# Opening of a three-part attention and expert kernel: loads reordered, queries of the first tile alone, the other three tiles' queries as units of the first batch

## The reference, cut to what matters

```
x = x + cross_attention(layernorm(x), ctx)    # x: 8 batches x 64 queries x 256; ctx: 8 x 1601 x 256; 16 heads of 16
x = x + causal_self_attention(layernorm(x))   # 64 tokens of each batch
x = x + experts(layernorm(x))                 # 8 experts of 256 -> 1024 -> 256, the best 2 of each token
q = layernorm(x) @ Wq.T + bq;  k = ctx @ Wk.T + bk;  v = ctx @ Wv.T + bv
cross_attention = (softmax(q k / 4) v) @ Wo.T + bo
```

## Time and profile before

| | |
|---|---|
| runs before | 703.81, 708.26, 1222.36 us; median 708.26 |
| profiled execution, its own time | 710.84 us |
| its span in the trace | 709.0 us, 16064 instructions |
| PE, DVE, ACT, POOL busy | 94%, 67%, 46%, 41% of the span |
| mean granted TensorE clock | 0.976 of full |

### The profile page before, as it was taken

How to read it: one execution, slowest core, us unless ns; L and a number is a source line. 1 busy time by engine, 2 the same in 40 slices (tenths; PEclk the granted TensorE clock), 3 DMA queues, 4 the chain that set the end, 5 groups by cost and what they waited for, 6 DMA issues and landing times.

```text
span 709.0 us, 16064 instructions
## 1 busy us (share of the span) xinstructions
PE 663.4 (94%) x6584; PEld 544.1 (77%) x6584; DVE 476.0 (67%) x868; ACT 324.3 (46%) x520; POOL 290.8 (41%) x384
## 2 busy tenths in 40 slices
PE   2979999999999999999999999888997999999997
PEld 2657877877877877877887886655786999999996
DVE  4695677657567887674977865667764766666753
ACT  2434554554554455455445544345444444444421
POOL 2004698797694678665678767200000000000000
PEclk9997999999999999999999999979997999999999
DMA  7210020120010011001001000052103033312000
GB/s 234 62 47 24 25 64 9 32 64 25 1 49 24 25 28 44 25 25 48 11 26 38 2 1 2 11 230 75 46 1 120 1 120 120 118 33 85 0 0 30
DMA packets 12500, 34.12 MB, mean 48 GB/s; under 512 B 1483, under 2 KB 9812, under 8 KB 10260
## 3 DMA queue, kind: packets, MB, share of 16 engines
q1 hardware_dynamic: 12180, 31.62, 13.6%
q0 software_dynamic: 256, 1.58, 0.6%
HBM read 32.67 MB, written 0.52 MB: 47 GB/s over the span
## 4 chain that ended last, share of the span: by engine, by line
PE 79%; DVE 9%; issue 5%; ACT 2%; POOL 2%; DMA 1%; SPq 0%; POOLq 0%; DVEq 0%; ACTq 0%
PE bank L1060 44%; PE bank L1224 13%; PE bank L1069 8%; PE bank L1120 5%; POOL prob_sum L444 2%; DVE maxes L800 2%; PE bank L1154 2%; PE bank L1163 2%; ACT probs L650 1%; DMA bias_sb<-in_biases 1%; DVE ctx_lo L740 1%; DVE prob_sum L444 1%; DVE shift L758 1%; PE bank L1138 1%; PE bank L1101 1%
## 5 line engine op out<-in xcount | busy, mean ns | idle before, releaser
L444 POOL TENSOR_TENSOR prob_sum<-probs,prob_sum 128x256 f32<-128x256 f32 x336 | 265.1, 820 | 81.8 <-ACT probs L650 77.8
L650 ACT ACTIVATE probs<-bank 128x1024 f32<-128x1024 f32 (+1 forms) x104 | 106.6, 1025 | 133.8 <-PE bank L1224 118.0
L800 DVE TENSOR_REDUCE maxes<-bank 128x1 f32<-128x400 f32 (+1 forms) x256 | 132.0, 566 | 23.7 <-PE bank L1120 21.6
L632 ACT ACTIVATE h_raw<-bank,b_sb 128x512 f32<-128x512 f32 (+2 forms) x72 | 46.1, 641 | 112.0 <-PE bank L1060 111.9
L781 DVE SCALAR_TENSOR_TENSOR k_lo<-bank,bias_sb,k_hi 128x400 fp32r<-128x400 f32 (+2 forms) x64 | 40.4, 632 | 55.0 <-ACT k_hi L553 54.9
L1224 PE MATMUL bank<-qbd_hi,k_hi 64*128 64x256 f32 (+1 forms) x416 | 73.0, 346 | 3.7 <-ACT probs L650 2.8
L1060 PE MATMUL bank<-w_hi,h_hi 128*128 128x256 f32 x256 | 72.9, 285 | 0.1
L1060 PE MATMUL bank<-w_hi,h_lo 128*128 128x256 f32 x256 | 72.4, 283 | 0.0
L1060 PE MATMUL bank<-w_lo,h_hi 128*128 128x256 f32 x256 | 72.3, 283 | 0.0
L1069 PE MATMUL bank<-probs,v_sb 128*32 128x128 f32 (+1 forms) x1664 | 68.3, 283 | 2.5 <-DVE masked L748 2.0
L994 DVE CAST h_hi<-h_raw 128x512 fp32r<-128x512 f32 (+2 forms) x72 | 28.5, 396 | 62.4 <-ACT h_raw L632 62.3
(11 more groups left out here) (158 smaller groups left out, 1409.9 us busy)
## 6 DMA issues: line engine op xcount, KB each, us to landing
raw<-in_w SPq DMA_DIRECT2D x16, 1024.0 KB, 6.9
ctx_raw<-in_ctx_t SPq DMA_DIRECT2D x16, 400.0 KB, 3.6
ctx_raw<-in_ctx_t SPq DMA_DIRECT2D x8, 402.0 KB, 3.6
ctx_raw<-in_ctx_t SPq DMA_DIRECT2D x8, 399.0 KB, 3.6
w_sb<-in_w_t POOLq DMA_DIRECT2D x1, 1280.0 KB, 8.9
x_all<-in_x SPq DMA_DIRECT2D x1, 512.0 KB, 3.8
w_raw<-in_w_t SPq DMA_DIRECT2D x1, 512.0 KB, 4.7
result<-x_all SPq DMA_DIRECT2D x1, 512.0 KB, 2.7
```

Of the source, the lines that this page charges most:

```text
L444: ins = engine.tensor_tensor(prob_sum[0:ROWS[k], cols], probs[0:ROWS[k], s % 2, cols], acc[0:ROWS[k]], ALU.add)
L632: nc.scalar.activation(h_raw[:, c % 2, 0:width], bank[:, at, 0:width], ACT.Gelu, bias=b1_sb[:, bass.ds(e, 1), c:c + 1].rearrange("p a b -> ...
L650: nc.scalar.activation(probs[0:ROWS[k], s % 2, :].rearrange("p (g n) -> p g n", g=G), bank[0:ROWS[k], 0:ROW_TILES, :], ACT.Exp, scale=SCAL ...
L800: nc.vector.tensor_reduce(maxes[:, g * PAIRS + j, c:c + 1], src[:, 0:width], AX.X, ALU.max).then_inc(read_dve, 1)
```

## The change

The loads of the start are put in another order and cut: x of tile 0 alone, then Wk, context chunk 0, identity, biases, context chunk 1, Wv; x of the other three tiles and `w_sb` 1 to 5 (with Wo and the weights of the self attention) come behind later chunks, the latter now on SyncE's queue and counted in `late_in`. The start makes layernorm, transposes and queries of tile 0 alone. The same work for tiles 1, 2 and 3 becomes units of tile 0: p1, p2, p3 (transposes) and r1, r2, r3 (query products) at the steps of `REST_CHAIN`, with their statistics on VectorE in step 0. Wv is split in step 2 of the opening. The order of units is written out in `FIRST_ORDER`; V8, V9 and V10 now stand around X0 and X1 in the last step. Chunk splits move: (1,0) behind `find_shift`, (1,1) and (1,2) into steps 0 and 1 of tile 0. The product of bo's folding (L1270) moves behind the opening, and `ident_bf` as well.

```diff
-CONST_DMAS, LATE_DMAS = 2, 6
-CONSTS_MADE = 4
+CONST_DMAS, LATE_DMAS = 2, 7
+CONSTS_MADE = 3
-FIRST_K = {0: [0, 1], 1: [2, 3], 2: [4, 5], 3: [6, 7]}
-FIRST_V = {1: [0], 2: [1], 3: [2, 3], 4: [4, 5], 5: [6, 7], 6: [8, 9], 7: [10]}
-FIRST_M = in_order({1: 2, 2: 2, 3: 3, 4: 3, 5: 2, 6: 2, 7: 2})
-FIRST_SPLIT = {0: [(0, 0), (0, 1)], 1: [(0, 2)], 2: [(0, 3)], 5: [(1, 0)], 7: [(1, 1)], 8: [(1, 2)]}
-FIRST_STEPS = 10
+FIRST_ORDER = [
+    [("K", 0)],
+    [("K", 1)],
+    [("M", 0), ("K", 2), ("M", 1), ("V", 0)],
+    [("M", 2), ("K", 3), ("M", 3), ("V", 1)],
+    [("M", 4), ("K", 4), ("M", 5), ("V", 2)],
+    [("M", 6), ("K", 5), ("M", 7), ("V", 3)],
+    [("M", 8), ("K", 6), ("M", 9), ("V", 4)],
+    [("M", 10), ("K", 7), ("M", 11), ("V", 5)],
+    [("M", 12), ("V", 6), ("M", 13), ("M", 14), ("V", 7), ("M", 15)],
+    [("V", 8), ("V", 9), ("X", 0), ("X", 1), ("V", 10)],
+]
+FIRST_STEPS = len(FIRST_ORDER)
+FIRST_SPLIT = {1: [(0, 1)], 3: [(0, 2)], 5: [(0, 3)], 9: [(1, 0)]}
+FIRST_V_SPLIT_AT = 2
+FIRST_TILE_SPLIT = {0: (1, 1), 1: (1, 2)}
+REST_STATS_AT = 0
+REST_CHAIN = {3: ["p1"], 5: ["r1"], 6: ["p2"], 8: ["r2"], 9: ["p3"], 11: ["r3"]}
 SHIFT_AT = KT - 1
 FIND_SHIFT_AT = KT - 3
 OWN_V = {0: 11, 1: 12}
...
         order += [kind for kind, _ in row]
     prologue.by_act = [k in READ_BY_ACT for k in order]
-    first = Units(prologue.total(), 2, None, after_shift=0)
...
         def _(sp):
-            sp.dma_start(x_all[:, :, :], x).then_inc(x_in, 16)
...
             sp.dma_start(bias_sb[:, :, :], biases).then_inc(consts_in, 16)
             load(0, 1)
+            sp.dma_start(w_raw[:, 1], w_t[:, 7]).then_inc(v_weights_in, 16)
             for dst, src in ((bo_sb[:, :], bo_row), (bg_sb[:, :], bg_row), (wg_sb[:, :, :], wg_t),
                              (b1_sb[:, :, :], b1), (b2_sb[:, :], b2), (causal_sb[:, :], causal)):
                 sp.dma_start(dst, src).then_inc(late_in, 16)
-            for c in range(2, NC):
-                load(0, c)
+            load(0, 2)
+            sp.dma_start(x_all[:, 1:TT, :], x[:, 1:TT, :]).then_inc(rest_in, 16)
+            load(0, 3)
+            sp.dma_start(w_sb[:, 1:6], w_t[:, 1:6]).then_inc(late_in, 16)
             for c in range(NC):
                 load(1, c)
...
-            pool.dma_start(w_sb[:, 1:6], w_t[:, 1:6]).then_inc(weights_in, 16)
...
@@ -520,17 +533,19 @@
                     b = 2 * t + bi
                     if not more == bi == 1:
                         sum_probabilities(nc.gpsimd, pool, b, k, s, SUM_PIECES)
+                    if t == 0 and s == REST_STATS_AT:
+                        inverse_root(2, 1, TT - 1)
...
+            def queries_hi(src, t):
+                for g in range(G):
+                    nc.scalar.activation(q_hi[:, 2 * t:2 * t + 2, g, :],
+                                         src[:, g * P:g * P + P].rearrange("p (b q) -> p b q", b=2),
+                                         ACT.Identity, bias=bias_sb[:, 0, g:g + 1]).then_inc(q_hi_done, 1)
             def unit(units, n, kind, u, t, b, parity):
+                if kind[0] == "r" and kind != "router":
+                    units.wait_filled(act, filled, n)
+                    queries_hi(bank[:, units.bank_of(n), :], int(kind[1]))
+                    return
...
-                for b, c in FIRST_SPLIT.get(k, []) if k else []:
+                for b, c in FIRST_SPLIT.get(k, []):
                     split_hi(b, c)
                 step(PROLOGUE, k, 0, 0, 0)
-            for b, c in FIRST_SPLIT[0]:
-                split_hi(b, c)
+            split_hi(0, 0)
             act.wait_ge(consts_in, CONST_DMAS * 16)
             act.wait_ge(consts_made, CONSTS_MADE)
             act.wait_ge(xt_psum, 1)
-            nc.scalar.activation(xn_all_t[:, :, :], bank[:, 0:DC, :], ACT.Copy).then_inc(xt_ready, 1)
+            nc.scalar.activation(xn_t[:, :, :].rearrange("p c n -> p (c n)"), bank[:, 0, 0:D], ACT.Copy)\
+                .then_inc(xt_ready, 1)
             prepare(0)
             act.wait_ge(q_psum, 1)
-            for g in range(G):
-                nc.scalar.activation(q_hi[:, :, g, :], bank[:, g, :].rearrange("p (b q) -> p b q", b=B),
-                                     ACT.Identity, bias=bias_sb[:, 0, g:g + 1]).then_inc(q_hi_done, 1)
+            queries_hi(bank[:, 1, :], 0)
...
+                    if is_first(b) and k in FIRST_TILE_SPLIT:
+                        split_hi(*FIRST_TILE_SPLIT[k])
...
+            def queries_lo(src, t, done):
+                dve.wait_ge(q_hi_done, G * t + G)
+                for g in range(G):
+                    nc.vector.scalar_tensor_tensor(
+                        out=q_lo[:, 2 * t:2 * t + 2, g, :], in0=src[:, g * P:g * P + P].rearrange("p (b q) -> p b q", b=2),
+                        scalar=bias_sb[:, 0, g:g + 1], in1=q_hi[:, 2 * t:2 * t + 2, g, :].bitcast(F32), op0=ALU.add,
+                        op1=ALU.subtract).then_inc(q_split if g < G - 1 else done, 1)
+                if kind[0] == "r" and kind != "router":
+                    queries_lo(src, int(kind[1]), read_dve)
+                    return
...
-            dve.wait_ge(x_in, 16)
-            for t in range(TT):
-                statistics(x_all[:, t, :], t)
-            nc.vector.tensor_scalar(var_eps[:, :], mean_var[:, :, 1], EPS, None, ALU.add).then_inc(stats_ready, 1)
-            dve.wait_ge(kv_weights_in, 16)
-            for w, hi, lo in ((0, wk_hi, wk_lo), (1, wv_hi, wv_lo)):
+            def variances(first, last):
+                for t in range(first, last):
+                    statistics(x_all[:, t, :], t)
+                nc.vector.tensor_scalar(var_eps[:, first:last], mean_var[:, first:last, 1], EPS, None,
+                                        ALU.add).then_inc(stats_ready, 1)
+            def split_weights(w, hi, lo):
                 link(nc.vector.tensor_copy(hi[:, :, :], w_raw[:, w]))
                 nc.vector.tensor_tensor(lo[:, :, :], w_raw[:, w], hi[:, :, :].bitcast(F32),
                                         ALU.subtract).then_inc(kv_weights_split, 1)
-            for t in range(TT):
-                normalize(xn_all[:, t, :], x_all[:, t, :], 1, xn_ready, t)
-            dve.wait_ge(consts_in, CONST_DMAS * 16)
-            nc.vector.tensor_copy(ident_bf[:, :], ident[:, :]).then_inc(consts_made, 1)
+            dve.wait_ge(x_in, 16)
+            variances(0, 1)
+            dve.wait_ge(k_weights_in, 16)
+            split_weights(0, wk_hi, wk_lo)
+            normalize(xn[:, :], x_all[:, 0, :], 1, xn_ready)
...
-                for b, c in FIRST_SPLIT.get(k, []):
-                    split_lo(b, c)
                 if k == FIRST_STEPS - 1:
                     dve.wait_ge(read_dve, PROLOGUE.total()[2])
                     find_shift()
+                if k == FIRST_V_SPLIT_AT:
+                    dve.wait_ge(v_weights_in, 16)
+                    split_weights(1, wv_hi, wv_lo)
+                for b, c in FIRST_SPLIT.get(k, []):
+                    split_lo(b, c)
                 for n, kind, u in PROLOGUE.at[k]:
                     unit(PROLOGUE, n, kind, u, 0, 0, 0)
+            split_lo(0, 0)
             prepare(0)
-            for g in range(G):
-                dve.wait_ge(q_hi_done, g + 1)
-                nc.vector.scalar_tensor_tensor(
-                    out=q_lo[:, :, g, :], in0=bank[:, g, :].rearrange("p (b q) -> p b q", b=B),
-                    scalar=bias_sb[:, 0, g:g + 1], in1=q_hi[:, :, g, :].bitcast(F32), op0=ALU.add,
-                    op1=ALU.subtract).then_inc(q_split, 1)
-            dve.wait_ge(weights_in, 48)
+            queries_lo(bank[:, 1, :], 0, q_split)
+            dve.wait_ge(weights_in, 32)
             link(nc.vector.tensor_tensor(row_mask[:, :], mask_sb[:, 0:RH], mask_sb[:, RH:HG], ALU.add))
             dve.wait_ge(q_split, G)
             spread_queries(0, 0)
...
+            nc.vector.tensor_copy(ident_bf[:, :], ident[:, :])
...
+                            dve.wait_ge(q_split, G + TT - 1)
+                            dve.wait_ge(read_dve, rest_queries_read)
...
+                    if t == 0 and s == REST_STATS_AT:
+                        dve.wait_ge(rest_in, 16)
+                        variances(1, TT)
+                    for kind in units.chain.get(s + 1, []):
+                        if kind[0] == "p":
+                            tile_of = int(kind[1])
+                            if tile_of > 1:
+                                n = next(n for j in range(s) for n, kind, _ in units.at[j] if kind == f"p{tile_of - 1}")
+                                units.wait_filled(dve, filled, n)
+                            normalize(xn[:, :], x_all[:, tile_of, :], 2, xn_ready, tile_of)
+                    if is_first(b) and k in FIRST_TILE_SPLIT:
+                        split_lo(*FIRST_TILE_SPLIT[k])
...
+            def own_queries_of(dst):
+                for g in range(G):
+                    for c in range(DC):
```

(46 more changed lines are left out.)

33 lines of the change are left out of this document (18 added, 15 removed).

## The result

The changed kernel took 703.04 us (median of 20 runs, 698.43 to 705.59) against 706.35 for the kernel before (20 runs, 703.68 to 710.98 but for one). That one execution took 1222.36 us, lies far outside the spread and does not count in the ratio. The ratio is 0.9949, with a 95% interval of 0.9927 to 0.9970: 3.3 us faster, clear of no change but only half of one per cent, where 10.7 were forecast and 692 to 704 against the earlier median of 708.3 was the range. The profiled execution took 704.59 us with a span of 702.7, against 710.84 and 709.0. So the two traces differ by 6.3 us and the medians by 3.3; both gaps, 10.7 to 6.3 and 6.3 to 3.3, have to be explained.

What follows compares the result with a forecast made beforehand. The opening delays everything behind it, its ten steps going at VectorE's pace. Gains of 10.9 and 2.6 less losses of 2.2, 0.3 and 0.3 gave 10.7 us: 700.1 from the profile, 697.6 from the median; 8-in-10 range 692 to 704.

Steps and rivals of the forecast that it cites:

- Loads and start: Opening: chunk 0 landed at 5.2 us, K0 from 7.1 to 9.1, first queries spread at 13.4 in place of 24.7.
- the factor of 1.24 to 1.5: First loads: bytes moved in all per byte queued for a load when it lands, applied at 367 GB/s.
- The rival of cut loads: Start: cut loads run one by one, landing 4 us later than counted; gain 6.7, 701.6 us; chance 0.06.
- The ten steps: Opening after the spread queries: VectorE sets the pace, 24.0 us of work plus 3.6 idle, ending at 41.0.
- the third rival: Ten steps: VectorE loses its idle time through evenly spread maxima, 3.4 us more; gain 14.1, 694.2 us; chance 0.10.
- The shift: From last maximum to first scores: 3.8 us in place of 4.2, first scores at 44.8 in place of 55.67.
- The clock at the first scores: TensorE's clock stays full, so the 5.2 us from 55.67 to 60.9 at half clock take 2.6 less.
- VectorE's lag: Batch 0, tile 0: VectorE's added 7.4 us fit its idle time; five banks carry the lag, some 0.3 us lost.
- p and r units: Batch 0: 1.11 us a tile on TensorE; p1, r1, p2, r2 in full steps 3 to 8 lose 2.2 us.
- they cost nothing as long as GpSimd is last: Batch 0, steps 9 and 11: p3 and r3 hide under GpSimd's sums; without that cover they cost 1.1 us.
- as before, only earlier: Sign expected in the profile: everything after step 13 unchanged except for coming earlier.
- The profile as base: 10.7 us taken off the profiled 710.84 gives 700.1; against the median of the runs, 708.3, it gives 697.6.

## Why the prediction was wrong, point by point

- **Loads and start: mis-sized.** "Chunk 0 ... at 5.2" was 7.3, and the queries were spread at 16.1, not 13.4. The later terms of the start were right within 0.6 us in sum (8.8 us from the landing to the spread queries, where 8.2 were worked out). K0 took 2.35 us where a K unit takes 1.3 later, near the 2.0 that the sum had for it at half clock, though the profile's row grants 1.00 there; only the durations show it. The step that failed is the factor of 1.24 to 1.5 between queued and moved bytes at 367 GB/s. By 7.3 us some 1490 KB had moved (81, 278 and 322 GB/s over 3, 3 and 1.3 us) for 786 queued, an estimated factor of 1.9, and the rate from 3 to 6 us was 278. With the later loads held back some 960 KB had moved by 6.35 us (87, 216 and 139 GB/s over 3, 3 and 0.35 us), an estimated factor of 1.2, but the rate from 3 to 6 us was 216. The prediction read the 367 as holding for "many loads queued, whatever their size"; no row of before shows cut loads, and these runs gave 216, 278 and 353. The rival of cut loads was right in direction and half right in size: 2.1 us later, where it gave 4. Its mechanism, loads that run one by one, is not what the trace shows, as several are under way at once. The Trainium skill's page DMA: Bandwidth & Descriptors (Bandwidth) has the rule that large loads are needed for the rate; the 353 GB/s with loads of 128 to 402 KB, several at once, do not bear it out as a limit here. The runs don't separate the short pieces from the pauses between issues. 2.7 us of the 10.7 went here.
- **The ten steps: right in the sum, by chance in its parts.** 24.0 of work and 3.6 of idle time, 27.6; 27.5 was measured, with half clock in a part. At full clock it is 1.6 less. That is not the third rival (idle time lost as the order spreads the maxima), since the kernel before, with the old order, is 1.3 us shorter there too when its clock stays full (28.9 and 27.5). At either clock the old and the new order take the same time within 0.3 us.
- **The shift: right.** 3.8 us in the sum, 43.7 to 47.5 measured, and the clock stayed full. With the units moved away it fell.
- **The clock at the first scores: right.** 8.15 us ahead of before at the first scores (10.9 less the 2.7 of the start) became 10.5 at the second exponential, so 2.3 where the sum had 2.6.
- **VectorE's lag: mis-sized.** "The five banks carry it, with some 0.3 lost." TensorE waited 1.3 us for the first maximum of step 1:

```profile
PE bank L1119 <- DVE maxes L838: 1.3, 1, 1.3
```

  VectorE's lag is the one that was worked out (51.4 for the end of split (1,1), and 2.7 later by the start: 54.1; 54.3 measured). But V12 in step 1 is the unit that needs the first maximum read, five behind it, and I had looked at the first M of step 2. V12's turn comes 0.9 us earlier, and 1.3 were lost; the third exponential is 1.5 us less ahead than the second. Moving the statistics took most of it away (1.2 us).
- **p and r units: right in size, wrong on the cover.** From the third exponential (9.0 us ahead of before) to the mark (6.6) 2.4 us were lost, with 2.2 + 0.3 in the sum. But moving more of these units under GpSimd's sums gained nothing: the same 2.4 us were lost with all of them in steps 7 to 12. So the sum's "they cost nothing as long as GpSimd is last" holds for p3 and r3 and not for three tiles' worth.
- **Behind tile 0: "as before, only earlier" failed.** 10.7 less 2.7 less 1.2 is 6.8, and the marks give 6.6. The medians give 3.3, because TensorE's clock in the last batch falls or doesn't fall from one execution to the next, at a price of up to 3.6 us there, and by the totals it does so more often in the changed kernel: 11 of its first 20 runs are above 702.7, while 3 of 19 of before lie in the group at 710.8 to 711.0. The profiles are few, but point the same way: at the wait for the gates the clock fell in one of two profiles of before and in all six of the changed kernel and its variants without products. With products in that wait the difference of the medians is 6.2. Shown: the place, the price, and that the gain returns when it is filled. Open: why the changed kernel, whose last batch issues the same work, meets the fall more often. All that is seen to differ there is when the stretch comes.
- **The profile as base.** The sum was made against an execution of the group near 711, 4.5 us above the median of 20. Both first profiles happened to be of the kind in which the clock falls in the last batch, so the difference of the traces was sound, but not typical.

## What to carry to other kernels

Cutting the first loads brings the start forward less than their bytes say. The rate that one window shows is no constant: it was 216, 278 and 353 GB/s for the same loads issued in three ways, so count with a range, and hold back what isn't needed yet. Work moved off the opening should keep VectorE's long operations out of the first full steps (1.2 us here). Another engine's cover has a size: GpSimd's sums hid one tile's units at the end of batch 0, and with all three tiles' there TensorE came last itself. A gain of under 1% can be hidden by a place far behind where the clock falls in some executions; compare marks in the trace, and fill that place. Then look in the trace at whether the added work lies in the wait: seven products that missed it by 2 us held nothing and cost 1.6 us.

## What the runs showed of the hardware

The same kernel, with 3.4 of 6 us of TensorE work in a stretch and no single wait above 2.0 us, was granted full clock behind it in one execution and 0.50 for about 10 us in another, 3.6 us apart by the end of the last batch. In the opening the same happened: 28.9 against 27.3 us for the same ten steps, and 28.9 against 27.5 in the kernel before. Seven products of 512 columns in the wait of 2 us for the gates went with a clock of 1.00 behind it in five of five profiles, against one of eight without them. At the start the matmuls of K0 took 0.54 us each and those of the same size some 4 us later 0.34, while the row of the granted clock read 1.00 over both.
